# A transformer layer on one core: the softmax shift rows are turned on VectorE and sent through DRAM, where TensorE turned them before

## What is computed

```python
qkv = x @ Wqkv + bqkv
scores = jnp.einsum('bqhd,bkhd->bhqk', q, k) / HD
prob = jax.nn.softmax(scores, axis=-1)
out = jnp.einsum('bhqk,bkhd->bqhd', prob, v)
x = _layernorm(x + out @ Wout + bout)
gate, up = jnp.split(x @ wq_gu.T, 2, axis=-1)
hn = rms_norm(silu(gate) * up)
x = _layernorm(x + hn @ wq_p.T)
```

## Time and profile before

| | |
|---|---|
| Median of 3 runs | 560.94 us (559.83 to 561.97) |
| The profiled execution | 563.55 us, of it a span of 561.6 us |
| Mean granted TensorE clock | 0.976 |
| Busy share: TensorE, VectorE, ScalarE, GpSimd | 93%, 78%, 65%, 60% |
| Mean DMA traffic | 88 GB/s |

### The profile page before, as it was taken

One profiled execution on the slowest core, in us unless ns is written; L12 is line 12 of the kernel. 1 busy time (PEld: TensorE's weight loads), 2 busy tenths in 40 slices (PEclk: granted clock), 3 DMA queues, 4 the chain that ended last, 5 costly groups with the idle time before them and its releaser, 6 DMA issues.

```text
span 561.6 us, 13548 instructions
## 1 busy us (share of the span) xinstructions
PE 524.3 (93%) x4148; PEld 446.9 (80%) x4148; DVE 440.3 (78%) x1002; ACT 365.1 (65%) x738; POOL 335.5 (60%) x517
## 2 busy tenths in 40 slices
PE   4787999999999999999999999999999999999883
PEld 4677778688888888888888888888888888777782
DVE  6867796767889787878787888888888888874763
ACT  4552774557677767676777667676767776767653
POOL 4566774244665756575755656566566574656863
PEclk9796999999999999999999999999999999999996
DMA  9777173615252635354453536262627062010001
GB/s 233 132 143 126 45 137 78 110 51 112 61 105 45 142 56 134 68 125 77 105 98 95 104 86 112 74 115 67 121 52 146 7 158 42 22 40 1 20 19 38
DMA packets 83379, 49.16 MB, mean 88 GB/s; under 512 B 39680, under 2 KB 83328, under 8 KB 83328
## 3 DMA queue, kind: packets, MB, share of 16 engines
q1 hardware_dynamic: 81584, 48.00, 41.2%
q10 hardware_dynamic: 1744, 0.53, 0.5%
HBM read 33.29 MB, written 14.68 MB: 85 GB/s over the span
## 4 chain that ended last, share of the span: by engine, by line
PE 72%; DVE 7%; POOL 6%; issue 6%; DMA 4%; ACT 2%; SPq 2%; ACTq 0%; POOLq 0%; DVEq 0%
PE ffn_ps L591 17%; PE short_ps L517 12%; PE down_ps L604 9%; PE pv_ps L619 9%; PE exp_ps L572 9%; PE short_ps L563 9%; DMA q_st<-shift_lo 2%; POOL sq_sum L1020 2%; PE short_ps L627 2%; DVE row_max L837 2%; POOL h_lo L1015 1%; PE ffn_ps L709 1%; PE ffn_ps L643 1%; PE short_ps L632 1%; PE short_ps L673 1%
## 5 line engine op out<-in xcount | busy, mean ns | idle before, releaser
L837 DVE TENSOR_REDUCE row_max<-short_ps 128x2 f32<-128x512 f32 x256 | 169.9, 681 | 38.3 <-PE short_ps L563 36.9
L1015 POOL TENSOR_TENSOR h_lo<-h_f,h_hi 128x256 fp32r<-128x256 f32 x128 | 94.6, 739 | 171.4 <-ACT h_hi L740 171.2
L764 ACT ACTIVATE probs<-exp_ps 128x1024 f32<-128x1024 f32 x128 | 130.7, 1021 | 43.1 <-PE exp_ps L572 42.7
L563 PE MATMUL short_ps<-k_st,q_st 65*128 65x256 f32 x512 | 108.4, 296 | 3.9 <-DVE row_max L837 3.4
L749 ACT ACTIVATE tanh<-ffn_ps 128x256 f32<-128x256 f32 x120 | 45.7, 381 | 90.8 <-PE ffn_ps L591 90.8
L563 PEld LDWEIGHTS short_ps<-k_st,q_st 65*128 65x128 f32 x512 | 88.4, 193 | 15.1 <-issue 3.0
L572 PE MATMUL exp_ps<-q_st,k_st 67*128 67x512 f32 x256 | 81.8, 401 | 4.0 <-DMA q_st<-shift_lo 3.7
L591 PE MATMUL ffn_ps<-x1T_hi,wguT 128*128 128x256 f32 x480 | 80.1, 289 | 3.8 <-DVE h_f L913 3.6
L604 PE MATMUL down_ps<-wpT,h_hi 128*128 128x256 f32 x256 | 79.6, 333 | 3.7 <-POOL h_lo L1015 3.5
L591 PE MATMUL ffn_ps<-x1T_lo,wguT 128*128 128x256 f32 x480 | 77.9, 285 | 0.0
L1020 POOL TENSOR_TENSOR sq_sum<-sq_sum,h_sq 128x256 f32<-128x256 f32 x105 | 77.4, 737 | 0.0
(11 more groups left out here) (104 smaller groups left out, 834.4 us busy)
## 6 DMA issues: line engine op xcount, KB each, us to landing
q_st<-q_dram SPq DMA_DIRECT2D x128, 128.0 KB, 3.9
q_dram<-q_p SPq DMA_DIRECT2D x16, 512.0 KB, 3.0
k_st<-k_dram SPq DMA_DIRECT2D x64, 64.0 KB, 2.3
res<-in_L_attn_x_dram SPq DMA_DIRECT2D x16, 256.0 KB, 2.9
out_dram<-y_out SPq DMA_DIRECT2D x16, 256.0 KB, 2.9
xn<-in_L_attn_x_dram SPq DMA_DIRECT2D x62, 64.0 KB, 2.7
wgu_raw<-in_L_ffn_w_gate_up_dram SPq DMA_DIRECT2D x8, 256.0 KB, 6.1
k_dram<-k_p SPq DMA_DIRECT2D x16, 128.0 KB, 2.5
```

The costliest lines, as they stand in the source:

```text
L563: last = pe.matmul(bank[:, t * S:(t + 1) * S], q_st[0:PAD, st.par, head, t * P:(t + 1) * P], k_st[0:PAD, st.par, st.s % 4, :], start=True, ...
L764: act.activation(probs[:, st.s % 4], exp_ps[:], ACT.Exp).then_inc(exp_done, 1)
L837: dve.tensor_reduce(row_max[:, st.par, head * TT:(head + 1) * TT], short(n, f"max{i}")[:].rearrange("p (t k) -> p t k", t=TT), AX.X, ALU.m ...
L1015: pool.tensor_tensor(h_p[1][:, st.s % 4, :], h_f[:, st.s % 2, :], h_p[0][:, st.s % 4, :].bitcast(F32), ALU.subtract).then_inc(h_lo, 1)
```

## The change

VectorE transposes `row_max` in blocks of 32 x 32, right after the last maximum of the half, in slots 12 and 16. Blockwise transposing leaves, in partition 32 g + c, column c of the 32 queries of block g. The split is done on that (128 x 32, from SBUF), and both parts lie in one tile `shift_p`. SP stores the tile to DRAM in the same slot (32 KB, 128 pieces of 256 bytes), waits in the next slot until this has landed, and reads each part back into its row of `q_st` (8 KB in 64 pieces of 128 bytes). TensorE's 32 turns and their uses of short PSUM banks are gone. VectorE clears `row_max` once at the start, since the first transpose reads all of it.

```diff
-SHIFT_T = (13, 17)
+SHIFT_SAVE = (12, 16)
+SHIFT_LOAD = (13, 17)
-SHIFT_SPLIT = (13, 17)
+SHIFT_SPLIT = (12, 16)
...
                 for half in range(2):
-                    if st := n.once(SHIFT_T[half]):
+                    if st := n.once(SHIFT_SAVE[half]):
                         sp_wait(shift_split, st.count(2, half + 1))
+                        sp.dma_start(shift_dram[half], shift_p[half][:].bitcast(F32)).then_inc(shift_saved[half], 16)
+                    if st := n.once(SHIFT_LOAD[half]):
+                        sp_wait(shift_saved[half], st.count(16, 16))
                         for part in range(2):
                             sp.dma_start(
                                 q_st[PAD + part:PAD + part + 1, st.par, half * H // 2:(half + 1) * H // 2, :]
-                                .bitcast(F32), shift_p[half][part][:].bitcast(F32)).then_inc(shift_loaded[half], 16)
+                                .bitcast(F32).rearrange("r h (t g j) -> r (h t) g j", t=TT, g=P // BLOCK),
+                                shift_dram[half, :, part:part + 1].rearrange("(g c) r j -> r c g j", c=H * TT)
+                                [:, half * H:(half + 1) * H]).then_inc(shift_loaded[half], 16)
...
-            def turn_maxima(bank, st, half):
-                wait(pe, max_taken, st.count(16, 8 * half + 8))
-                pe.transpose(bank[0:H * TT // 2, 0:P], row_max[:, st.par, half * H:(half + 1) * H], ident[:]
-                             ).then_inc(shift_turned, 1)
...
             def shift_rows(n, st, half):
-                src = short(n, f"shift{half}")[0:H * TT // 2, 0:P]
-                hi, lo = shift_p[half]
+                hi, lo = shift_p[half][:, 0], shift_p[half][:, 1]
+                wait(dve, max_taken, st.count(16, 8 * half + 8))
+                wait(dve, shift_split, st.count(2, half))
+                dve.transpose(shift_t[:], row_max[:, st.par]).then_inc(shift_turned, 1)
                 wait(dve, shift_turned, st.count(2, half + 1))
                 wait(dve, shift_loaded[half], st.count(32, 0))
```

More of the change, by code:

```diff
@@ L74 @@
 RSTD2 = 44
-SHORT_ORDER = ("max0", "q", "max1", "sq", "k", "shift0", "o", "shift1", "v", "x1")
-SHORT_OFFSET = {"v": PROJ_V, "q": PROJ_Q, "shift0": SHIFT_T[0], "shift1": SHIFT_T[1],
-                "o": PROJ_O, "k": PROJ_K, "x1": X1_T, "sq": SUM_SQ}
+SHORT_ORDER = ("max0", "q", "max1", "sq", "k", "o", "v", "x1")
+SHORT_OFFSET = {"v": PROJ_V, "q": PROJ_Q, "o": PROJ_O, "k": PROJ_K, "x1": X1_T, "sq": SUM_SQ}
 SHORT_USES = [(m, name) for m in range(SLOTS) for name in SHORT_ORDER
@@ L81 @@
 BANK_TABLE = {0: {"max0": 2, "max1": 0, "sq": 1},
-              1: {"max0": 2, "max1": 0, "shift1": 1},
+              1: {"max0": 2, "max1": 0},
               2: {"max0": 0, "max1": 2, "q": 1, "o": 0},
@@ L85 @@
               4: {"max0": 0, "max1": 2, "k": 1},
-              5: {"max0": 2, "max1": 1, "shift0": 0, "x1": 2},
+              5: {"max0": 2, "max1": 1, "x1": 2},
               6: {"max0": 0, "max1": 1},
@@ L281, in postln_layer @@
         row_max = sb("row_max", [P, 2, H * TT])
-        shift_p = [[sb(f"shift{h}_{n}", [H * TT // 2, P], F32R) for n in ("hi", "lo")] for h in range(2)]
+        shift_t = sb("shift_t", [P, H * TT])
+        shift_p = [sb(f"shift_p{h}", [P, 2, H * TT], F32R) for h in range(2)]
+        shift_dram = nc.dram_tensor("shift_dram", [2, P, 2, H * TT], F32)
         probs = sb("probs", [P, 4, TT, 2, S])
@@ L350, in postln_layer @@
         shift_turned, shift_split = sem("shift_turned"), sem("shift_split")
-        shift_hi = sem("shift_hi")
+        shift_hi, maxima_cleared = sem("shift_hi"), sem("maxima_cleared")
+        shift_saved = [sem(f"shift_saved{i}") for i in range(2)]
         shift_loaded = [sem(f"shift_loaded{i}") for i in range(2)]
@@ L531, in turn_weights @@
                 last.then_inc(w_tr, 1)
-            released_by = {"v": (v_copied, 1, 1), "q": (q_read, 1, 1), "shift0": (shift_split, 2, 1),
-                           "shift1": (shift_split, 2, 2),
-                           "o": (r1_done, 1, 1), "k": (k_copied, 1, 1), "x1": (x1T_lo, 1, 1),
+            released_by = {"v": (v_copied, 1, 1), "q": (q_read, 1, 1), "o": (r1_done, 1, 1), "k": (k_copied, 1, 1), "x1": (x1T_lo, 1, 1),
                            "sq": (ms_done, 1, 1)}
@@ L680, in slot @@
                     last.then_inc(k_made, 1)
-                if st := n.once(SHIFT_T[0]):
-                    bank = use_short(n, "shift0")
-                    turn_maxima(bank, st, 0)
                 if st := n.once(PROJ_O):
@@ L692, in slot @@
                     last.then_inc(o_made, 1)
-                if st := n.once(SHIFT_T[1]):
-                    bank = use_short(n, "shift1")
-                    turn_maxima(bank, st, 1)
                 keep_clock(n, 2)
@@ L823, in _ @@
             dve.memset(k_st[SROWS:XROWS].bitcast(F32), 1.0).then_inc(k_ones, 1)
+            dve.memset(row_max[:], 0.0).then_inc(maxima_cleared, 1)
+            dve.wait_ge(maxima_cleared, 1)
             def low(dst, src, hi):
@@ L833, in take_maximum @@
                 wait(dve, max_scored, st.count(16, 2 * st.s + i + 1))
-                if st.s == 0 and i == 0:
-                    wait(dve, shift_turned, st.count(2, -2))
                 head = first_head(st.s) + 4 * i
@@ L840, in shift_rows @@
             def shift_rows(n, st, half):
-                src = short(n, f"shift{half}")[0:H * TT // 2, 0:P]
-                hi, lo = shift_p[half]
+                hi, lo = shift_p[half][:, 0], shift_p[half][:, 1]
+                wait(dve, max_taken, st.count(16, 8 * half + 8))
+                wait(dve, shift_split, st.count(2, half))
+                dve.transpose(shift_t[:], row_max[:, st.par]).then_inc(shift_turned, 1)
                 wait(dve, shift_turned, st.count(2, half + 1))
                 wait(dve, shift_loaded[half], st.count(32, 0))
-                dve.tensor_scalar(hi[:], src, -1.0, None, ALU.mult).then_inc(shift_hi, 1)
+                dve.tensor_scalar(hi, shift_t[:], -1.0, None, ALU.mult).then_inc(shift_hi, 1)
                 wait(dve, shift_hi, st.count(2, half + 1))
-                dve.scalar_tensor_tensor(lo[:], src, -1.0, hi[:].bitcast(F32), ALU.mult, ALU.subtract
+                dve.scalar_tensor_tensor(lo, shift_t[:], -1.0, hi.bitcast(F32), ALU.mult, ALU.subtract
                                          ).then_inc(shift_split, 1)
@@ L914, in slot @@
                                       ).then_inc(h_done, 1)
-                if st := n.once(SHIFT_SPLIT[0]):
-                    shift_rows(n, st, 0)
                 if (st := n.chunk(H_LOW0)) and st.s and sums_on_dve(st):
@@ L927, in slot @@
                     take_maximum(n, st, 1)
+                for half in range(2):
+                    if st := n.once(SHIFT_SPLIT[half]):
+                        shift_rows(n, st, half)
                 if st := x_turn(n):
@@ L936, in slot @@
                     tern_weights(c)
-                if st := n.once(SHIFT_SPLIT[1]):
-                    shift_rows(n, st, 1)
                 if st := n.once(MEAN_SQ):
```

## The result

The changed kernel takes 599.98 us at the median of 4 runs (596.01 to 602.32), the kernel before 560.38 us beside it. The ratio is 1.069 (95% interval 1.066 to 1.073): 39.6 us slower at the medians, where 20.6 us were forecast and 597 us was the upper end of the range. The profiled execution has a span of 594.2 us, 32.6 us more than before.

The account below looks back on a forecast made before the run. TensorE's list was taken as the bound, every wait paid in full. Late shift rows +22.5, keys +1.5 and the second half's turns -3.4 sum to +20.6 us on 560.94, forecasting 581.5 us, range 566 to 597 us.

Parts of the forecast that it names:

- the largest term: First half, phase 7: exp_scores waits for the shift rows through DRAM, 1.5 us in 15 batches, +22.5 us.
- the sum of +20.6 us: Whole program: 22.5 for late shift rows, 1.5 for keys, less 3.4 for the second half's turns.
- So there the turn that is gone counts: 16 x 0.21 = -3.4 us: Second half on TensorE: rows come in time, so removing its turn gains 0.21 us in each of 16 batches.
- This makes 10 us on an engine at 78%, beside TensorE. I cost it at nothing.: VectorE: 32 new transposes at 0.3 us each run beside TensorE's work and cost nothing.
- the cover (TensorE's work): VectorE's added transposes run beside TensorE; if that cover were gone, they would cost 10 us.
- 15 x 1.5 = +22.5 us.: Phase 7: from keys' store to last shift load takes 6.1 us, TensorE allows 4.6; 15 batches come 1.5 us later.
- the loads' 2.1 us: Last 8 KB shift load from DRAM: taken as 2.1 us, between ends of 1.8 and 2.7 us.
- my low end: Shift rows' 32 KB store to DRAM: low end 1.8 us, high end 3.0, taken as 2.4.
- I take 1.5 us for the whole program: Phase 1: SP's new wait delays the keys' loads, a second TensorE wait of up to 0.6 us in some batches.
- Rival 4, the clock: TensorE: waits slow its clock, 3 us more per batch with long DMA ends, +82, 643 us; chance 0.05.
- The second half has no wait: Second half: shift rows are there at 327.5, exp scores need them only past 328.5, so TensorE does not wait.
- The estimate from the page: Shift path from the Trainium skill: two DMA legs of 2.0 us, 5.6 us path, delay 1.0, total about 573 us.

Follow-up runs that it names:

- the version with all places mended: Changed kernel with first-half shift store before keys' store, input loads after keys' and queries', VectorE shift work behind pvT, second half's work and store a slot later: 571.52 us.
- the one with both edits and the moved loads: Changed kernel with first-half shift store before keys' store, VectorE shift work behind pvT, input loads behind keys' and queries' loads: 577.83 us (1.030).

## Why the prediction was wrong

The sign, the mechanism of the largest term and the place of the second were right. The size was not, and the sum of +20.6 us hid errors of both signs.

- **"So there the turn that is gone counts: 16 x 0.21 = -3.4 us"**. This is the step that failed first. I took the turn's share of the chain for its worth. It is nothing that can be measured: without it the ratio is 1.002 (0.9995 to 1.004). The evidence was in the chain of before, where `down` takes 0.67 us right behind the products with the values and 0.47 us behind a turn; I had read the one row and not its neighbour.
- **"This makes 10 us on an engine at 78%, beside TensorE. I cost it at nothing."** This is the step that cost most. In total VectorE's new work is small (the three instructions together measured 13.0, 7.1 and 6.8 us, a mean of 0.84 us per half), but in phase 0 it stands between the last maximum and `pvT`, for which TensorE waits in the same slot. Alone it costs 13.7 us; in the changed kernel, where other waits lie beside it, phase 2 has 7.6. I had also sized each split at under 0.3 us, and one of them took 0.65 us in phase 0 (more on it below). I had named the cover (TensorE's work) without asking who waits for the instruction behind.
- **"15 x 1.5 = +22.5 us."** The mechanism was right, and moving the store in SP's list took 20 us off. The size was too large: 15.8 us in phase 7, 0.82 us in the batch shown instead of 1.5. Of the legs, 0.82 from keys' store to shift store was forecast as 0.87, and the loads' 2.1 us was right. The store landed in 1.9 us in phase 4 of this batch, near my low end, and this is the term that was mis-sized; its median of 2.4 mixes that with the second half's, which is behind the queries (434.54 to 437.98).
- **"I take 1.5 us for the whole program"** for the keys. 4.2 us by phase, but removing it alone gave 0.1 us, since `pvT` was as late.
- **Rival 4, the clock**, with 0.05: it happened three times in the program, not each batch. After the waits that end at 80.04, 298.81 and 490.55 the clock was at a mean of 0.71, 0.66 and 0.68 for about 5 us, between its two levels (0.50 is 1.2 GHz, 1.00 is 2.4 GHz), and the next distances were 1.3, 1.6 and 1.6 us longer, nearly all of phase 0's 5.2. The waits before were 2.97, 2.28 and 1.47 us long, and I had tied the fall to waits near 3 us. That the waits brought the fall is read from the traces, not tested:

```profile
299.00:304.00 5.00, 5.00 (x35) 3.98 (x35) 1.67 (x4) 1.63 (x3) 1.41 (x2) 0.66 0.58 128
...
490.50:495.90 5.40, 5.35 (x36) 3.94 (x37) 1.17 (x4) 1.63 (x3) 1.41 (x2) 0.68 0.83 146
```

- **The second half has no wait**: right in the changed kernel.
- **The estimate from the page** has a slip: 560.9 + 15 x 1.0 + 1.5 - 3.4 is 574, not 573. The Trainium skill (DMA: Bandwidth & Descriptors, Anatomy of one DMA) gives its 2.0 us for DMAs that GpSimd issues, while SP issues these. Even so its two legs of 2.0 us agree with the 1.9 and 2.1 us measured here, and its delay of 1.0 us was nearer to the 0.82 us than my 1.5.

So the forecast's terms of +22.5, +1.5 and -3.4 us were +15.8, +4.2 and about 0, and two terms that it put at nothing were +7.6 (VectorE) and +5.2 us (phase 0, the clock).

The phases sum to 32.7 us for the profiled executions. The 39.6 us between the medians hold some 7 us more: the profiled execution of the changed kernel was the fastest of its four at 596.0, 4.0 us below their median, and that of the kernel before (563.55) was 3.2 us above its median. The other three runs have mean granted clocks of 0.963 to 0.966, against 0.971 in the profiled one, so more such stretches are likely in them; no trace of them exists, and this part stays open.

## What to carry to other kernels

An instruction's share of the chain need not be what its removal gives: look at the same neighbours with and without it elsewhere in the trace. An engine with a fifth of its time free can still bound a slot, so for every instruction that is put ahead of another, name who waits for that other. A hop through DRAM costs its landings only once they pass the slack, but its issue queues behind whatever waits on the same sequencer, and there the place in the list was worth 20 us. Of parallel waits, remove them together or expect nothing.

## What the hardware showed beside this

- After 16 products with 32-column weights at different places of the array, the next weight load started 0.41 us after the last of theirs had ended, whether it was 16 or 128 columns wide. In a stretch of low clock (behind 490.55) it was 0.81 us. One small product fitted there for free: that is the turn, 0.9995 to 1.004 without it.
- The same 128 x 32 `tensor_scalar` on VectorE took 0.18 us in phase 4 and 0.65 us in phase 0. In phase 0 it began at 433.57, while a GpSimd operation ran from 433.45 for 0.73 us, and it ended at 434.22, when that had ended; in phase 4 it ran from 418.83 to 419.01, and GpSimd was idle until 419.18. The transposes beside it took 0.21 us both times:

```profile
433.45 0.73 POOL L1011 TENSOR_TENSOR h_lo<-h_f,h_hi 128x256 fp32r<-128x256 f32 x1 [2.79 <-ACT h_hi L735]
```

  So it goes in all 32 executions of this `tensor_scalar` in the changed kernel. The 13 without a GpSimd operation beside them took 0.18 us each. Of the other 19, 17 took 0.30 to 0.91 us and ended 0.03 to 0.04 us behind the GpSimd operation, and 2 began in its last 0.1 us and took 0.18.

  The Trainium skill (SBUF — State Buffer, Who interferes with whom) says that VectorE's two-port mode and GpSimd contend: whoever issues first holds the shared ports for its whole instruction, and the other is blocked until then. This trace agrees as far as the blocking goes; no row shows in which mode the instruction ran. No run here took GpSimd's operation away, so the cause is read, not tested.
- The length of a wait did not by itself tell whether TensorE's clock would fall. In the changed kernel the clock fell after waits of 2.97, 2.28 and 1.47 us, and stayed at 1.00 after waits of 1.32 (109.75) and 1.14 us (332.14). In the version with all places mended it stayed at 1.00 after 2.46 us (68.70); in the one with both edits and the moved loads it was at a mean of 0.66 after 1.22 us (293.37). These two stretches, first the one behind 2.46 us:

```profile
68.70:73.70 5.00, 5.00 (x41) 4.00 (x42) 3.87 (x8) 2.13 (x3) 1.90 (x3) 1.00 0.39 126
```

```profile
293.37:298.37 5.00, 5.00 (x33) 3.36 (x34) 1.98 (x5) 1.63 (x3) 1.41 (x2) 0.66 0.83 159
```
